# Splitting two weight tensors ahead of the jobs, with gathers put ahead, pair loads on two queues and nine unread matmuls on TensorE, in a CIN tower on one core

## What is computed

```python
# x: (b, 39, 16)
prev = x
for k in range(3):
    z = einsum('bmd,bhd->bdmh', x, prev).reshape(b, 16, 39 * h)
    t = transpose(einsum('bdc,co->bdo', z, ws[k]) + bs[k])   # (b, 128, 16)
    t = t / sqrt(sum(t * t, axis=(-2, -1)))
    logit.append(t)
    prev = t
z = sum(concatenate(logit, axis=1), axis=-1)                 # (b, 384)
h = relu(concat([z, dense_ctx]) @ W_top1 + b_top1)
h = relu(h @ W_top2 + b_top2)
y = h @ W_top3
```

## Time and profile before

| What | Value |
|---|---|
| Median of 3 runs (lowest, highest) | 1120.15 us (1119.07, 1122.03) |
| The profiled execution, its own time | 1120.02 us |
| Its span, first to last instruction | 1118.3 us |
| TensorE busy, matmuls | 1049.8 us (94%), x4376 |
| VectorE busy | 939.6 us (84%) |
| GpSimd busy | 900.5 us (81%) |
| ScalarE busy | 814.0 us (73%) |
| Mean granted TensorE clock over the span | 0.989 |
| DMA queues: q1 (SyncE's), q10 (ScalarE's), q0 (gathers) | 32.81 MB, 5.96 MB, 1.29 MB |

### The profile page before, as it was taken

One profiled execution on the slowest core, in us unless ns is written; L12 is line 12 of the kernel. 1 busy time (PEld: TensorE's weight loads), 2 busy tenths in 40 slices (PEclk: granted clock), 3 DMA queues, 4 the chain that ended last, 5 costly groups with the idle time before them and its releaser, 6 DMA issues.

```text
span 1118.3 us, 17869 instructions
## 1 busy us (share of the span) xinstructions
PE 1049.8 (94%) x4376; PEld 788.5 (71%) x4376; DVE 939.6 (84%) x3189; ACT 814.0 (73%) x2756; POOL 900.5 (81%) x726
## 2 busy tenths in 40 slices
PE   0696999999999999999999999999999999999999
PEld 0364677777777777777777777777777777778773
DVE  2285789899889989899998989999898998898892
ACT  2464587877878787787868777786878778788872
POOL 6586698888989888888988888888888888677770
PEclk9898999999999999999999999999999999999999
DMA  5513022020203002030302102020300203000000
GB/s 157 131 48 100 2 74 51 7 68 3 71 3 72 3 7 67 3 71 3 72 3 46 29 4 71 3 71 3 66 8 8 66 3 72 1 1 1 1 1 0
DMA packets 57166, 41.18 MB, mean 37 GB/s; under 512 B 37963, under 2 KB 40907, under 8 KB 56934
## 3 DMA queue, kind: packets, MB, share of 16 engines
q1 hardware_dynamic: 49522, 32.81, 12.2%
q10 hardware_dynamic: 2420, 5.96, 1.7%
q0 software_dynamic: 5120, 1.29, 1.5%
HBM read 38.09 MB, written 1.94 MB: 36 GB/s over the span
## 4 chain that ended last, share of the span: by engine, by line
PE 58%; POOL 26%; ACT 7%; issue 5%; DMA 2%; DVE 1%; SPq 1%; POOLq 0%; ACTq 0%; DVEq 0%
POOL sums L307 20%; PE acc L598 9%; PE bank_a L533 9%; PE bank_a L535 8%; PE bank_a L534 8%; PE bank_d L533 7%; PE bank_d L535 7%; PE bank_d L534 7%; POOL gathered L295 5%; ACT scaled L423 5%; ACT t L447 1%; DMA x_pairs<-x_scratch 1%; ACT squares L450 1%; PE turned L574 1%; PE bank_a L652 1%
## 5 line engine op out<-in xcount | busy, mean ns | idle before, releaser
L307 POOL TENSOR_TENSOR sums<-sums,scaled 128x512 f32<-128x512 f32 x512 | 686.7, 1342 | 141.8 <-ACT scaled L423 107.3
L723 DVE SCALAR_TENSOR_TENSOR sums<-bank_d,x_col,sums 128x128 f32<-128x128 f32 x2176 | 626.5, 339 | 108.8 <-PE bank_d L535 66.4
L423 ACT ACTIVATE scaled<-bank_a,x_col 128x128 f32<-128x128 f32 x2048 | 585.9, 382 | 153.0 <-PE bank_a L535 146.4
L533 PE MATMUL bank_a<-w_hi,prev_lo 128*128 128x512 f32 x640 | 283.1, 442 | 21.1 <-ACT scaled L423 8.9
L533 PE MATMUL bank_d<-w_hi,prev_lo 128*128 128x512 f32 (+1 forms) x640 | 278.0, 434 | 5.5 <-DVE sums L742 5.4
L535 PE MATMUL bank_a<-w_hi,prev_hi 128*128 128x512 f32 x640 | 254.4, 398 | 0.0
L534 PE MATMUL bank_a<-w_lo,prev_hi 128*128 128x512 f32 x640 | 253.8, 396 | 0.0
L535 PE MATMUL bank_d<-w_hi,prev_hi 128*128 128x512 f32 (+1 forms) x640 | 245.6, 384 | 0.0
L534 PE MATMUL bank_d<-w_lo,prev_hi 128*128 128x512 f32 (+1 forms) x640 | 245.4, 383 | 0.0
L423 ACT ACTIVATE sums<-bank_a,x_col 128x128 f32<-128x128 f32 x512 | 146.7, 372 | 70.5 <-PE bank_a L535 70.5
L295 POOL DMA_INDIRECT gathered<-in_table,idx x160 | 169.4, 1059 | 30.9 <-issue 19.2
(11 more groups left out here) (57 smaller groups left out, 470.5 us busy)
## 6 DMA issues: line engine op xcount, KB each, us to landing
x_pairs<-x_scratch SPq DMA_DIRECT2D x144, 156.0 KB
x_pairs<-x_scratch SPq DMA_DIRECT2D x80, 78.0 KB
gathered<-in_table,idx POOLq DMA_INDIRECT x160
w_raw<-in_w ACTq DMA_DIRECT2D x3, 448.0 KB
x_scratch<-gathered SPq DMA_DIRECT2D x16, 72.0 KB, 2.2
w_raw<-in_w ACTq DMA_DIRECT2D x3, 384.0 KB
w_raw<-in_w ACTq DMA_DIRECT2D x1, 1024.0 KB
w_raw<-in_w ACTq DMA_DIRECT2D x1, 768.0 KB
```

The costliest lines, as they stand in the source:

```text
L307: nc.gpsimd.tensor_tensor(out=sums[:, n % SUMS, :, :], in0=sums[:, n % SUMS, :, :], in1=scaled[:, a - 1, :, :], op=ALU.add).then_inc(a_add ...
L423: op = nc.scalar.activation(to[:, i, :], bank_a[at % A_RING][:, i * UNITS:(i + 1) * UNITS], ACT.Copy, scale=x_of(c, q, a * PER_BANK + i))
L533: nc.tensor.matmul(to, lo, w_h, start=True, stop=False)
L723: nc.vector.scalar_tensor_tensor(out=taken(n, u) if u in LEFT else total, in0=taken(n, u), scalar=x_of(c, q, A_FIELDS + u), in1=total, op0 ...
```

## The change

- **Weights.** ScalarE's queue issues all of w1 (three parts, a semaphore each), then w0, the biases, all of w2 (three parts) and the top biases, with no wait between them. ScalarE rounds the three pieces of w1 and the first three of w2, waits for chunk 0's scratch stores, issues five of the fourteen pair loads of chunk 0 (groups 1 and 3; SyncE keeps 0 and 2), and rounds the other three pieces of w2. VectorE waits for `ones_made`, which GpSimd sets behind chunk 0's gathers, then subtracts w1's pieces and three of w2's; one more comes behind chunk 0's z, two more behind the first `low`. Nothing of w2 is left in the jobs.
- **Gathers.** `start_chunk(2)` and chunk 2's first three gathers stand ahead of `low(1, 0)`. In jobs 0 to 2 stand the other seven.
- **Matmuls.** TensorE runs three matmuls of `ones` by raw w1 (`keep_busy`, 128x512, float32) once chunk 0's scratch is stored, two after chunk 0's pair matmuls, four after its norm. They write bank_d0, and nobody reads it before it is overwritten.

```diff
@@ -124,2 +124,8 @@
-W2_PARTS = [(0, 7), (7, 14), (14, 21), (21, 27), (27, 33), (33, 39)]
-W1_PARTS = [(0, 16), (16, 28), (28, 39)]
+W_LOADS = {1: [(0, 16), (16, 28), (28, 39)], 2: [(0, 14), (14, 27), (27, 39)]}
+W_PIECES = {1: [(0, 16), (16, 28), (28, 39)], 2: [(0, 7), (7, 14), (14, 21), (21, 27), (27, 33), (33, 39)]}
+GATHERS_BEFORE = 3
+W2_FIRST, W2_SECOND = 3, 4
+SP_GROUPS, ACT_GROUPS = [0, 2], [1, 3]
@@ -213 +219 @@
-        w_loaded = {k: sem(f"w{k}_loaded") for k in (1, 2)}
+        w_loaded = {k: [sem(f"w{k}_loaded{part}") for part in range(len(W_LOADS[k]))] for k in (1, 2)}
@@ -263,0 +270,16 @@
+        def load_pairs(queue, c, p):
...
@@ -328,0 +351,3 @@
+            start_chunk(2)
+            for j in range(GATHERS_BEFORE):
+                gather(2, j)
@@ -338 +363,3 @@
-                if it + 2 < CHUNKS and place == 0:
+                if it == 0:
+                    first += GATHERS_BEFORE
+                elif it + 2 < CHUNKS and place == 0:
@@ -362,15 +388,0 @@
-            def load_pairs(c, p):
...
@@ -385,2 +397,2 @@
-                for p in range(NP):
-                    load_pairs(c, p)
+                for p in range(NP) if c else SP_GROUPS:
+                    load_pairs(sp, c, p)
@@ -404,2 +416,4 @@
-            def split_high(k, part, lo, hi):
-                act.wait_ge(w_loaded[k], 16 * (part + 1))
+            def split_high(k, piece):
+                lo, hi = W_PIECES[k][piece]
+                part = [first <= lo < last for first, last in W_LOADS[k]].index(True)
+                act.wait_ge(w_loaded[k][part], 16)
@@ -465,0 +480,7 @@
+            raws = {1: w1, 2: w2}
+            def load_raw(k):
+                for part, (lo, hi) in enumerate(W_LOADS[k]):
+                    act.dma_start(w_raw[k][:, lo:hi, :], raws[k][:, lo:hi, :]).then_inc(w_loaded[k][part], 16)
+            load_raw(1)
@@ -470,7 +491 @@
-            for part, (lo, hi) in enumerate(W1_PARTS):
-                if part:
-                    act.wait_ge(w_loaded[1], 16 * part)
-                act.dma_start(w_raw[1][:, lo:hi, :], w1[:, lo:hi, :]).then_inc(w_loaded[1], 16)
-            for part, (lo, hi) in enumerate(W1_PARTS):
-                split_high(1, part, lo, hi)
-            act.wait_ge(pairs_loaded[NP - 1], PAIR_LOADS[NP - 1] * 16)
+            load_raw(2)
@@ -480 +495,9 @@
-            act.dma_start(w_raw[2][:, 0:W2_PARTS[0][1], :], w2[:, 0:W2_PARTS[0][1], :]).then_inc(w_loaded[2], 16)
+            for piece in range(len(W_PIECES[1])):
+                split_high(1, piece)
+            for piece in range(W2_FIRST):
+                split_high(2, piece)
+            act.wait_ge(scratch_stored, 48)
+            for p in ACT_GROUPS:
+                load_pairs(act, 0, p)
+            for piece in range(W2_FIRST, len(W_PIECES[2])):
+                split_high(2, piece)
@@ -489,6 +511,0 @@
-                if n < len(W2_PARTS):
-                    lo, hi = W2_PARTS[n]
-                    split_high(2, n, lo, hi)
-                    if n + 1 < len(W2_PARTS):
-                        lo, hi = W2_PARTS[n + 1]
-                        act.dma_start(w_raw[2][:, lo:hi, :], w2[:, lo:hi, :]).then_inc(w_loaded[2], 16)
@@ -614,0 +632,6 @@
+            def keep_busy(count):
+                for _ in range(count):
+                    nc.tensor.matmul(bank_d[0][:, :], ones[:, :], w_raw[1][:, 0:4, :].rearrange("p m u -> p (m u)"),
+                                     start=True, stop=True)
@@ -616,0 +640,3 @@
+            pe.wait_ge(w_loaded[1][0], 16)
+            pe.wait_ge(scratch_stored, 48)
+            keep_busy(3)
@@ -620,0 +647 @@
+            keep_busy(2)
@@ -621,0 +649 @@
+            keep_busy(4)
@@ -688,2 +716,3 @@
-            def split_low(k, part, lo, hi):
-                dve.wait_ge(w_hi_made[k], part + 1)
+            def split_low(k, piece):
+                lo, hi = W_PIECES[k][piece]
+                dve.wait_ge(w_hi_made[k], piece + 1)
@@ -799,2 +828,6 @@
-            for part, (lo, hi) in enumerate(W1_PARTS):
-                split_low(1, part, lo, hi)
+            dve.wait_ge(ones_made, 1)
+            for piece in range(len(W_PIECES[1])):
+                split_low(1, piece)
+            for piece in range(W2_FIRST):
+                split_low(2, piece)
@@ -802,0 +836,2 @@
+            for piece in range(W2_FIRST, W2_SECOND):
+                split_low(2, piece)
@@ -808,0 +844,3 @@
+            dve.wait_ge(prev_lo_made[1], 1)
+            for piece in range(W2_SECOND, len(W_PIECES[2])):
+                split_low(2, piece)
@@ -834,2 +871,0 @@
-                    if u == 18 and n < len(W2_PARTS):
-                        split_low(2, n, *W2_PARTS[n])
```

More of the change, by code:

```diff
@@ L262, in x_of @@
             return x_col[:, c % 3, q, m:m + 1]
+        def load_pairs(queue, c, p):
+            rows = scratch[c, :, :].rearrange("(m b) e -> m (b e)", b=CB)
+            tiles = PAIR_GROUPS[p]
+            for kk in range(PER_TILE):
+                at = slice(kk * FIELDS, (kk + 1) * FIELDS)
+                if p == 0:
+                    queue.dma_start(x_rep[at, :], rows[0:FIELDS, :]).then_inc(pairs_loaded[p], 16)
+                offsets = [PAIR_OFFSETS[PER_TILE * i + kk] for i in tiles if PER_TILE * i + kk < OFFSETS]
+                if offsets:
+                    first = rows[offsets[0]:offsets[0] + FIELDS, :]
+                    window = bass.AP(first.tensor, first.offset,
+                                     [[ROWS, FIELDS], [PER_TILE * ROWS, len(offsets)], [1, ROWS]])
+                    queue.dma_start(x_rot[at, tiles[0]:tiles[0] + len(offsets), :],
+                                    window).then_inc(pairs_loaded[p], 16)
         def bdim(ap):
@@ L543, in bank_for_act @@
                     m = a * PER_BANK
-                    pe.wait_ge(w_lo_made[1], 1 + sum(m >= lo for lo, _ in W1_PARTS[1:]))
+                    pe.wait_ge(w_lo_made[1], 1 + sum(m >= lo for lo, _ in W_PIECES[1][1:]))
                 if (k, c, q) == (2, 0, 0) and a == 0:
-                    pe.wait_ge(w_lo_made[2], len(W2_PARTS))
+                    pe.wait_ge(w_lo_made[2], len(W_PIECES[2]))
                 if q == 0 and a == 0:
```

19 lines of the change are left out of this document (3 added, 16 removed).

## The result

The changed kernel takes 1113.28 us (median of 6 runs, 1112.11 to 1114.62), the kernel before, run beside it, 1120.91 us (6 runs). The ratio is 0.9934, 95% interval 0.9921 to 0.9947. So it is faster, by 7.6 us, where 13.9 were forecast; 1113.28 lies just outside the range, above its upper end of 1113.0. The profiled execution has a span of 1110.4 us for 1118.3, a difference of 7.9.

What follows compares the result with a forecast made beforehand. It took TensorE as the bound, busy 197.33 of 200 us in the steady stretch, with losses in early waits. Its terms summed to -13.9 us, span 1118.3 to 1104.4, predicted time 1106.1 us, range 1099 to 1113.

Steps and rivals of the forecast that it cites:

- Term a: Start of the jobs: GpSimd ready at 46.1 us, TensorE's first bank at 47.5 for 45.65, +1.9 us (-0.3 to +5).
- pair loads on two queues, costed at nothing: Start: z and prev_hi may come 2 to 3 us earlier, but GpSimd is last to be ready, so no gain.
- if prev_lo of chunk 0 waits for ScalarE and not for gathers: Sign at the first prev_lo that would show the forecast wrong.
- The held instructions: Start: gathers held while VectorE's added weight subtractions run, +1.2 us (0 to 4).
- The idle matmuls: Start: TensorE idles again after the last dummies, half clock at the first job as before, zero gain.
- Term b: Jobs: splits leaving ScalarE and VectorE save TensorE's 0.41 us wait at 79.00, -0.4 us (0 to -0.4).
- Term c: Jobs: shorter gathers bring chunk 1's prev_lo sooner, shrinking TensorE's 1.87 us wait, -0.7 us (0 to -1.9).
- Terms d, e and f: TensorE's wait behind GpSimd's adds -3.9, its wait for chunk 2's z -6.2, half clock behind these waits -2.8 us.
- z's remainder of 0.8 us: Chunk 2's pair matmul: 0.8 us of the 7.00 us wait for z was to stay.
- Term g: TensorE's wait at 133.64 for prev_lo of (2, 0) and its half clock: half goes, -1.8 us (0 to -3.6).
- Rival 1: Start later than thought, with 3 us of the z wait left: 1110.7 to 1115.2 us, chance 0.20.
- Rival 4: Start: index loads wait for the whole weight queue, indices at 26.7 us, about 1125 us in all, chance 0.06.

Runs made afterwards that it cites:

- experiment 2: Changed kernel with all fourteen pair loads of chunk 0 on SyncE's queue, none on ScalarE's: 1110.17 us, ratio 0.9904 to the kernel before.
- experiment 3: Changed kernel without its nine idle matmuls: 1114.23 us, ratio 0.9941 to the kernel before.
- experiment 6: Kernel before with only three of chunk 2's gathers put ahead of the first prev_lo: 1111.44 us, ratio 0.9910; with descriptor space doubled too, 1110.27 us.
- Experiment 5: Changed kernel with GpSimd's descriptor space at 8192 instead of 4096: 1110.7 us, ratio 0.9909; with 2048, 1112.92 us, ratio 0.9925.
- experiment 4: Changed kernel with four of chunk 2's gathers ahead of the first prev_lo, the others two a job: 1116.53 us, ratio 0.9959.
- experiment 1: Changed kernel with ScalarE issuing no weight load before SyncE's two small index loads have landed: 1112.89 us, ratio 0.9928.
- experiment 8: Changed kernel with indices and identity first, one pair-load queue, later subtractions, w2 loaded behind first prev_hi, split in jobs, five gathers ahead, 8192 descriptor space: 1102.9 us.
- the last kernel: experiment 8 with two w1 subtractions behind chunk 0's pair products, w2 loaded by SyncE and its pieces done by job 3: 1103.27 us, ratio 0.9839.
- experiment 7's first run: Changed kernel with indices and identity first, one pair-load queue, subtractions and w2's loads held until chunk 0's gathers land: 1110.52 us, ratio 0.9909.

## Why the prediction was off

Its sum was -13.9, the measured change of the span is -7.9. By its terms:

- **Term a, the start: +1.9 forecast, +4.3 measured** at the first transpose, +5.7 at the first bank. Two steps failed. The first is "pair loads on two queues, costed at nothing": the second queue cost 2.8 us up to the first z and 2.3 us at the first bank (experiment 2), and the cover named for it, GpSimd as the last to be ready, was not there. By my own test ("if prev_lo of chunk 0 waits for ScalarE and not for gathers") the step was wrong, with 2.45 us of waiting. The second is a size: GpSimd was ready at 47.50, not at 46.1, mainly because the index loads came 2.6 us later, for 1. The held instructions are 1.2 us, as forecast, but 1.0 of it lies in the identity and the index add (2.40 and 1.69 us) and 0.2 in chunk 1's ten gathers. The three extra gathers with their index add took 5.2 us, as forecast. From the first bank to the first transpose it is 1.4 us shorter than before, of which experiment 3 puts 0.9 down to the clock.
- **The idle matmuls: forecast to do nothing.** Wrong by 0.9 us behind the first bank (experiment 3); more is not shown.
- **Term b, splits out of the jobs: -0.4 forecast, -0.6 measured** from the first to the second transpose. Right: with the splits left in (experiment 6) this stretch is 8.4 us as before, for 7.7.
- **Term c, the wait for prev_lo of chunk 1: -0.7 forecast, +4.3 measured.** This is the largest miss. The step said that a prev_lo behind fewer held gathers comes sooner. It left out a resource that the trace of before shows, in the 2.07 us before the gather at 90.82, which I took for part of a gap that would close. Moving three gathers forward moved this pause from behind prev_lo to ahead of it; the wait grew from 1.87 to 4.07 us, and half clock followed, 2.1 us more. Experiment 5 shows both gone with a larger descriptor space: a wait of 2.23 us, and 9.42 us for the stretch that took 9.45 before. So the forecast gain of 0.7 was not there either.
- **Terms d, e and f: -12.9 forecast, -14.3 measured** in the two stretches between the third and fifth transpose. The waits went as forecast, z's remainder of 0.8 us as well. That last part was right for a wrong reason: TensorE was held earlier. With that hold shortened, z costs 0.92 to 4.77 us again (experiments 4 and 5). So of terms c and e one is bought with the other.
- **Term g, -1.8 forecast, -1.7 measured** at the seventh transpose, by the clock rather than by the wait: 1.98 us are left of 2.25.

The misses in a (+2.4) and c (+5.0), less 1.4 for d to f, are the 6.0 us. Rival 1 (start later) came nearest in time, but for its reason only in part: the weights did not hold chunk 0's gathers (they landed 2.0 us after the last issue). They would have, had the indices been early (experiment 1). Rival 4, indices behind the whole weight queue, did not happen. On the place where I weighed a rule against a row, the trace speaks for the row: gathers beside the subtractions took 2.21 and 1.61 us, for 0.95 without. The Trainium skill, SBUF — State Buffer, "Who interferes with whom", infers that such work leaves descriptor generation alone; by that these two would have stayed at 0.95.

What stays open: why the pair matmuls run at half clock for longer in some executions than in others (7.87 to 9.35 us with the idle matmuls, 7.95 to 9.16 without); what decides whether a GpSimd instruction is held for one subtraction or for all that follow; and how much of experiment 8's gain each of its parts has; only the sum was run.

## What to carry to other kernels

When work is moved forward on a queue, list what recurs by count and not by place, such as a wait for descriptor space every so many gathers, and ask behind or ahead of which critical instruction it will now stand. Ask of each bulk load whether anything small and urgent uses the DMA engines at the same time; loading weights early is not free, and in this kernel the first chain became fast when w2's moved later. Try the smallest part of a change by itself: here six lines brought all of its gain.

## What the runs showed of the hardware

- GpSimd pauses first before its 15th indirect gather of 128 rows with 2048 of descriptor space and before its 29th with 4096; with 8192 not before the 58th. The pauses are 0.8 to 2.6 us in quiet stretches and 5.91 beside pair loads. Not every one is seen: in experiment 4, where the gathers stand apart, the 29th does not pause, and with 2048 the 58th does not.
- Beside back-to-back two-input VectorE subtractions an instruction of GpSimd is sometimes held for one of them (identity 2.40 us for 0.29, index add 1.69 for 0.21, in the changed kernel) and sometimes for all (identity 8.82 beside six, experiment 1; index add 4.47 beside two, the last kernel; a gather 4.23 for 0.95 beside three, experiment 7's first run).
- Gathers and small stores that run beside bulk weight loads complete late: gathers 6.8 us after the last issue for 1.3, stores 8.5 for 1.9.
- Loads spread over two queues delay their first part: the first of four groups is ready after 8.8 us for 6.1, and the last no sooner.
- A TensorE wait of 4.07 us took the granted clock to 0.50 from 87.8 us on, and it stayed there for 5.4 us of work behind the wait. Of shorter waits some did this and some did not: 2.23 us (experiment 5) and 1.98 at 126.97 did not, 2.25 in the earlier trace rows and 1.97 in the last kernel did (first matmul 0.76 and 0.77 us for 0.47). The fall can also come late: behind the 3.51 us of experiment 8 the first matmul took 0.47 us, and the granted clock was 0.63 from 122 to 126 us.
